# Dots of the second network's first two units made by TensorE from turned rows instead of by VectorE, in a two-network graph kernel

## The reference

```
h = relu(layernorm(x)); x = x + elu(softmax(mask(leaky(f1[:,None] + f2[None,:]))) @ h)
                        # f1, f2 = h @ W_fc.T @ a1, a2
y = relu(layernorm(x))
for l in range(3):
    si = y @ attn_w[l, :256]; sj = y @ attn_w[l, 256:]       # the dots
    attn = softmax(mask(leaky(si[:, None] + sj[None, :] + attn_b[l])))
    h = layernorm(y + attn @ y) * g1[l] + beta1[l]
    y = layernorm(h + gelu(h @ W1[l] + b1[l]) @ W2[l] + b2[l]) * g2[l] + beta2[l]
out = x + y
```

## Time and profile before

| | us |
|---|---|
| median of 3 runs (lowest, highest) | 2795.41 (2794.3, 2795.49) |
| profiled execution, its own time | 2794.51 |
| its span | 2792.7 |
| TensorE busy | 2668.0 (96%) |
| VectorE busy | 2301.8 (82%) |
| ScalarE busy | 2147.8 (77%) |
| GpSimd busy | 1692.1 (61%) |

### The profile page before, as it was taken

How to read it: one execution, slowest core, us unless ns; L and a number is a source line. 1 busy time by engine, 2 the same in 40 slices (tenths; PEclk the granted TensorE clock), 3 DMA queues, 4 the chain that set the end, 5 groups by cost and what they waited for, 6 DMA issues and landing times.

```text
span 2792.7 us, 53529 instructions
## 1 busy us (share of the span) xinstructions
PE 2668.0 (96%) x16868; PEld 2390.7 (86%) x16868; DVE 2301.8 (82%) x8507; ACT 2147.8 (77%) x3982; POOL 1692.1 (61%) x2197
## 2 busy tenths in 40 slices
PE   3599999999999999999999999999999999999997
PEld 2388989898888898898888898989888999999997
DVE  5999888889888888888888888888988777777774
ACT  4588888878787878787877787878777876776774
POOL 4656655656766565666666665655666644544655
PEclk7599999999999999999999999999999999999999
DMA  6221122212222221222221212121323111111111
GB/s 188 93 75 54 65 76 65 71 61 86 83 96 69 66 73 52 80 65 83 79 97 59 80 65 76 56 80 45 102 80 99 54 52 52 35 52 52 50 63 53
DMA packets 118014, 201.34 MB, mean 72 GB/s; under 512 B 12736, under 2 KB 85472, under 8 KB 117728
## 3 DMA queue, kind: packets, MB, share of 16 engines
q1 hardware_dynamic: 117728, 197.87, 21.8%
HBM read 113.95 MB, written 83.89 MB: 71 GB/s over the span
## 4 chain that ended last, share of the span: by engine, by line
PE 70%; DVE 14%; POOL 7%; issue 5%; ACT 3%; DMA 0%; DVEq 0%; POOLq 0%; SPq 0%; ACTq 0%
PE bank L569 33%; PE bank L554 26%; PE ps_u L528 5%; DVE g_lo L917 3%; DVE st L891 3%; POOL xo L358 3%; PE ps_u L610 2%; PE ps_s L523 2%; POOL rs L1198 2%; DVE ub L972 1%; POOL hb L358 1%; DVE ub L1002 1%; PE ps_s L515 1%; DVE vb L886 1%; ACT g_hi L792 1%
## 5 line engine op out<-in xcount | busy, mean ns | idle before, releaser
L569 PE MATMUL bank<-w_hi,g_hi 128*128 128x256 f32 x3072 | 891.7, 290 | 19.0 <-DVE g_lo L917 18.2
L569 PE MATMUL bank<-w_hi,g_lo 128*128 128x256 f32 x3072 | 865.0, 282 | 0.0
L569 PE MATMUL bank<-w_lo,g_hi 128*128 128x256 f32 x3072 | 863.6, 281 | 0.0
L792 ACT ACTIVATE g_hi<-bank,b_eff 128x512 fp32r<-128x512 f32 x768 | 529.0, 689 | 432.8 <-PE bank L554 427.4
L917 DVE TENSOR_TENSOR g_lo<-bank,g_hi 128x512 fp32r<-128x512 f32 x768 | 517.7, 686 | 178.3 <-ACT bank L794 165.7
L554 PE MATMUL bank<-zt_hi,w_hi 128*128 128x512 f32 x1536 | 646.6, 421 | 7.1 <-DVE g_lo L917 3.7
L554 PE MATMUL bank<-zt_hi,w_lo 128*128 128x512 f32 x1536 | 607.1, 395 | 0.0
L554 PE MATMUL bank<-zt_lo,w_hi 128*128 128x512 f32 x1536 | 606.1, 395 | 0.0
L569 PEld LDWEIGHTS bank<-w_hi,g_hi 128*128 128x128 f32 x3072 | 578.5, 188 | 30.5 <-DVE g_lo L917 29.2
L569 PEld LDWEIGHTS bank<-w_lo,g_hi 128*128 128x128 f32 x3072 | 579.1, 189 | 0.8
L569 PEld LDWEIGHTS bank<-w_hi,g_lo 128*128 128x128 f32 x3072 | 578.3, 188 | 0.0
(11 more groups left out here) (95 smaller groups left out, 4291.7 us busy)
## 6 DMA issues: line engine op xcount, KB each, us to landing
xb<-x_scratch SPq DMA_DIRECT2D x88, 512.0 KB, 4.0
x_scratch<-xo SPq DMA_DIRECT2D x64, 512.0 KB, 4.8
xin<-in_x SPq DMA_DIRECT2D x40, 512.0 KB, 4.6
r_scratch<-elu_r SPq DMA_DIRECT2D x32, 512.0 KB, 3.1
xin<-r_scratch SPq DMA_DIRECT2D x32, 512.0 KB, 4.6
out<-xo SPq DMA_DIRECT2D x32, 512.0 KB, 3.3
m<-m_scratch SPq DMA_DIRECT2D x96, 128.0 KB, 3.7
x_scratch<-h SPq DMA_DIRECT2D x24, 512.0 KB, 2.9
```

Source lines behind the costliest of these rows:

```text
L569: mm = pe.matmul(y, g[:, c, r * P:(r + 1) * P], w[:, l, c, :], start=(c == 0 and n == 0), stop=(c == C - 1 and n == 2))
L792: act.activation(g_hi[:, c, :], block_in, ACT.Gelu, bias=bias).then_inc(g_hi_ready, 1)
```

## The change

The dots of units 0 and 1 (steps -3 and -2) are no longer made by VectorE's eight instructions each. TensorE transposes the eight 128 x 128 blocks of the new rows into `bank[0]` and `bank[2]`, ScalarE copies them to SBUF (into `ub`, under the name `ht`), TensorE multiplies them with a two-column operand `aw_col`, and VectorE copies the 8 resulting columns to `dots`. VectorE's copy is put behind its `mask_sums` and `low_halves`. Two loads of 256 single elements each are added for `aw_col`, ahead of the raw weights of layer 0. All later units keep VectorE's dots.

```diff
+        aw_col = sb("aw_col", [P, K1, 2])
...
+        def turned_dots(s):
+            return s < -1
+        def turned_set(s):
+            return s + 3
+        ht = ub.rearrange("p t d -> p (t d)").rearrange("p (k n) -> p k n", k=K1)
...
                 sp.dma_start(b1_col[:, :, :], b1.rearrange("l (c p) -> p l c", p=P),
                              allow_slow_non_contiguous=True).then_inc(const_in, 16)
+                for j in range(2):
+                    sp.dma_start(aw_col[:, :, j], attn_w[0, j * D:(j + 1) * D].rearrange("(k p) -> p k", p=P),
+                                 allow_slow_non_contiguous=True).then_inc(const_in, 16)
                 raw_weights(0)
...
-                pe.wait_ge(const_in, 16 * 3)
+                pe.wait_ge(const_in, 16 * 5)
...
+                def turned_rows(rows, vec, n):
+                    for k in range(K1):
+                        for t in range(T):
+                            mm = pe.transpose(bank[2 * k][:, t * P:(t + 1) * P], rows[:, t, k * P:(k + 1) * P],
+                                              ident[:, :])
+                    mm.then_inc(ht_ps, 1)
+                    pe.wait_ge(ht_ready, K1 * (n + 1))
+                    for t in range(T):
+                        for k in range(K1):
+                            mm = pe.matmul(bank[1][:, 2 * t:2 * t + 2], ht[:, k, t * P:(t + 1) * P], vec[:, k, :],
+                                           start=(k == 0), stop=(k == K1 - 1))
+                    mm.then_inc(hdots_ps, 1)
+                def next_turned():
+                    if turned_dots(s) and live(s + 3):
+                        pe.wait_ge(x_made, st.nth0(s + 3))
+                        if live(s + 2):
+                            pe.wait_ge(dots_ready, st.nth(s + 2, 2 * T))
+                        turned_rows(xb[(s + 3) % 2], aw_col, turned_set(s))
...
                     if -4 <= s <= -2:
                         bias_shifts(s + 4)
+                    next_turned()
                     row_turns()
                     turns()
...
-                act.wait_ge(const_in, 16 * 3)
+                act.wait_ge(const_in, 16 * 5)
...
+                def turned_rows():
+                    if turned_dots(s) and live(s + 3):
+                        n = turned_set(s)
+                        act.wait_ge(ht_ps, n + 1)
+                        if n:
+                            act.wait_ge(hdots_ps, n)
+                        for k in range(K1):
+                            act.activation(ht[:, k, :], bank[2 * k][:, :], ACT.Copy).then_inc(ht_ready, 1)
...
                     elus()
+                    turned_rows()
                     turned()
                     if -4 <= s <= -2:
                         high_halves(s + 4)
...
+                def turned_copy(dot, n, ready):
+                    dve.wait_ge(hdots_ps, n + 1)
+                    dve.tensor_copy(dot[:, :, :], bank[1][:, 0:2 * T].rearrange("p (t j) -> p j t", j=2)).then_inc(
+                        ready, 2 * T)
                 def next_dots(graphs):
-                    if live(s + 3):
+                    if live(s + 3) and turned_dots(s):
+                        turned_copy(dots[(s + 3) % 2], turned_set(s), dots_ready)
+                    elif live(s + 3):
...
                     elu_sums()
-                    next_dots(range(T))
-                    if sums_early:
+                    if turned_dots(s) and sums_early:
                         mask_sums(v0)
                     if -4 <= s <= -2:
                         low_halves(s + 4)
+                    next_dots(range(T))
+                    if not turned_dots(s) and sums_early:
+                        mask_sums(v0)
                     return
```

More of the change, by code:

```diff
@@ L195, in build @@
         v_ps = sem("v_ps")
+        ht_ps = sem("ht_ps")
+        ht_ready = sem("ht_ready")
+        hdots_ps = sem("hdots_ps")
         pro = sem("pro")
@@ L532, in body @@
                 s = st.s
-                v1, v2 = middle(s), late(s)
+                v0, v1, v2 = early(s), middle(s), late(s)
                 l = layer(s)
```

## The result

The changed kernel took 2806.51 us (median of 6 runs, 2805.16 to 2808.18) against 2795.19 for the kernel before (2794.3 to 2796.22): 1.004 times, 95% interval 1.003 to 1.005. So it is 0.4% slower, and outside the range of the prediction, which said 2791.6.

A forecast was written before the change was run, and what follows sets the result against it. TensorE, busy 96% of the span, was taken as the bound, with VectorE bounding the fill. 3.75 + 0.8 - 0.7 = 3.85 us earlier, carried to the end from 2795.41, gave 2791.6 us; range 2788.0 to 2795.8.

The forecast's parts named there:

- the last of the sum: From the end of the fill to the kernel's end: the 3.85 us gained is carried through unchanged.
- C: Step -4: each new single-element load stalls the queue 2.61 us, 5.2 in all; slower, 2796.1 us; chance 0.07.
- D: Step -2: turned path not hidden, GpSimd at 1.6 throughout, root 3.6 us late; time 2796.0 us; chance 0.06.
- E: Step 0: clock rise stays in time while work moves forward, up to 3 us back; about 2794.5 us; chance 0.05.
- if what is gained by 137 us is not what is gained at the end: After the fill: a stated sign that the prediction is wrong, with no size given.
- Step -4, 0.7 lost: The two added loads ahead of the raw weights delay x and VectorE's statistics: 0.7 us lost, bounds 0 and 1.1.
- Step -3, 3.75 gained: Unit 0: without VectorE's dots the score reduction starts at 76.4 instead of 80.14, 3.75 us gained, bounds 3.2 and 4.3.
- Step -2, 0.8 gained: Unit 1: GpSimd's low halves and mask decide, root for unit 0 at 112.8 instead of 113.39; 0.8 gained, bounds -0.1 and 2.3.
- the narrow products: TensorE's eight products for the dots: 1.3 us with hand-overs, bounds 0.95 and 1.97, priced by the bias products.
- ScalarE's wait ahead of `turned`: Step -2: ScalarE stands 2.4 us for unit 0's weight turns; its high halves start at 99.8 instead of 96.11.

The follow-up runs named there:

- first kernel: Changed kernel with `aw_col` allocated behind all other SBUF tensors, so every other tensor keeps its address of the kernel before: 2792.58 us (0.9992).
- eighth kernel: As the seventh kernel, with the two `aw_col` loads issued at step -3 behind layer 1's raw weights, with their own semaphore: 2788.39 us (0.9975).
- seventh kernel: Changed kernel with `aw_col` last and unit 0's weight turns and their copies ahead of unit 1's turned rows: 2788.11 us (0.9978).
- the sixth: Changed kernel with `aw_col` last, only unit 0's dots from turned rows, unit 1's dots on VectorE in the old order: 2794.67 us (0.9999).
- fifth: Kernel before with 32 unused bytes ahead of `w1_hi`, so weights, g and zt all move together: 2794.76 us (0.9999).
- eleventh: Changed kernel with 32 unused bytes ahead of `w1_hi`, the first tensor: 2806.71 us (1.0041).
- ninth: The seventh kernel with 64 unused bytes ahead of `g_hi` and 64 more ahead of `zt_hi`: 2772.1 us (0.9915).
- tenth: Kernel before with only 64 unused bytes ahead of `g_hi` and 64 more ahead of `zt_hi`: 2778.64 us (0.9937).

## Why the prediction was wrong

**The step that failed** is the last of the sum: "From there all engines start by the same amount earlier, and I take it to the end unchanged", with its ground at the start, "The change touches no instruction from step -1 on, so that part can only start earlier or later". It touches no instruction, but it does touch their operands' addresses. That costs 0.217 us in each of the last 16 steps (26.440 - 26.223), 0.083 in the longer ones from unit 23 to 79, and the whole is the difference between the changed kernel and the same with `aw_col` last: 2806.51 - 2792.58 = 13.9 us. None of the rivals had it. C and D looked for a loss in the fill, where the loads cost 0.4 to 1.0 us and step -2 gave 1.0 less than forecast. E is taken up below.

The prediction had named this as a sign of being wrong ("if what is gained by 137 us is not what is gained at the end"), but gave it no price and no chance.

**Without that**, the forecast of 2791.6 stands beside 2792.58. That looks better than it is. The sum said 3.85 us earlier at the end of the fill, and the traces show 1.8 (changed kernel) and 2.3 (first kernel), about half; the median gained 2.4, with an interval from 4.8 faster to 0.6 slower. So the terms erred too, some against each other. From the trace of the changed kernel:

- *Step -4, 0.7 lost.* The statistics start 0.65 us later (37.33), of which 0.26 was there from the first TensorE product on. At step -3 the lag behind the kernel before is 1.16, since the x of that step landed later by half a microsecond. Six traces with this part unchanged have the statistics at 36.51 to 36.94, six with the loads added at 37.10 to 37.42. The eighth kernel puts the loads' price at 0.8. The term is about right; the half microsecond at step -3 was not in the sum.
- *Step -3, 3.75 gained.* From the last elu sum to the score reduction it takes 7.02 us (69.85 to 76.87); before, 11.45 (68.69 to 80.14). Gained: 4.4. The low halves took 1.60 and 1.30 where I took 1.70 each. But 1.3 of it is given back at once: from the reduction to the making of unit 1's rows the changed kernel takes 11.67 us, the kernel before 10.39. GpSimd's low halves end at 81.2, as before (81.5) and as forecast ("near 80 to 82"). But VectorE's small operations come 3.3 us sooner and now run beside them, and a 128x4 operation with two SBUF inputs takes 0.64 us there and 0.16 when they are over (L908 above). The working had no price for that. Net 3.1.
- The Trainium skill says of the port pair that VectorE and GpSimd share that it "is an **exclusive lock**, not a bandwidth split" ("SBUF — State Buffer", section SBUF: two separate sides): each waits for the whole of the other's instruction. The trace agrees for these: the three operations from 77.85 us on came every 0.69 us, which is one GpSimd instruction (5.52 us for 8). It does not agree for GpSimd's mask behind them, a single instruction of 1.93 us from 81.44: beside it one such operation took 0.59 and the next two 0.16 each, so they did not wait for its end. The measurement decides; what differs in the mask stays open.
- *Step -2, 0.8 gained.* Measured: 0.2 lost. The lead was 1.99 us when unit 1's rows were begun (88.54 against 90.53) and 1.82 at the shift (112.81 against 114.63). The mis-sized term is the narrow products, 3.57 us instead of 1.3, which makes ScalarE's copy and all behind it about 2 us late; GpSimd's low halves, 7.43 where the working had 8.5, gave 1.1 of that back. Two errors are in it. The 32 records of the bias products are 16 products of the program (8 chunks by 2 halves), two records each, and not 32 products as "The kernel before" says, so that eight products make 16 records. And the bias products ran at nearly full clock, 0.119 us a record; these ran at the low level, 0.223. The windows of the kernel before and of the changed kernel (after the busy times: granted clock, DMA share, GB/s):

```profile
54.30:58.10 3.80, 3.80 (x33) 3.73 (x31) 1.46 (x4) 2.14 (x8) 3.73 (x6) 0.93 1.01 318
```

```profile
70.50:74.00 3.50, 3.13 (x15) 3.13 (x15) 2.37 (x4) 3.50 (x5) 3.38 (x3) 0.50 0.77 310
94.50:98.40 3.90, 3.56 (x17) 3.56 (x18) 0.61 (x2) 0.29 (x1) 3.14 (x4) 0.50 0.00 0
```

  TensorE had been idle for 7.9 us ahead of the transposes in the first case, and the clock was at 1.2 GHz. A run of these products alone at either level was not made.
- *What was right there:* the order of events. ScalarE's wait ahead of `turned`, the late high halves, GpSimd's low halves (7.43 us, between the bounds of 5.50 and 9.4) and its mask as what the root waits for. The seventh kernel shows that wait's price: removed, unit 1's copy comes 3.6 us earlier (5.88 against 2.28).

**The rival on the clock** (E) said that the rise to full clock in step 0 would stay where it is in time. It moved with the work, from the 3 us after 134 (0.65) to the 3 us after 131 (0.63), after which the changed kernel ran at 1.00. Windows of the kernel before and of the changed kernel:

```profile
134.00:137.00 3.00, 3.00 (x10) 2.37 (x10) 3.00 (x11) 0.00 (x0) 1.28 (x2) 0.65 0.29 108
```

```profile
134.00:137.00 3.00, 2.95 (x18) 2.36 (x18) 3.00 (x11) 1.86 (x3) 0.00 (x0) 1.00 0.85 263
```

What the clock did cost came in single spells later. The changed kernel lost 1.5 us between units 5 and 6 that the kernel before did not. In the chain its first 24 products there took 4.37 us against 2.84, and the granted clock was 0.76 in those 7 us:

```profile
257.00:264.00 7.00, 5.13 (x31) 5.08 (x31) 4.99 (x29) 5.09 (x10) 3.95 (x5) 0.76 0.05 19
```

The kernel before had such a spell at 1481 to 1489 us (0.79), where the changed kernel had none. With one each, they cancel in this pair of traces and explain nothing of the 11 us. Other kernels had theirs elsewhere, and the sixth a longer one of 2.8 us, so a difference of 1 to 3 us between two single traces can be this alone.

## What to carry to other kernels

When a kernel is bound by TensorE for most of its time, adding an SBUF tensor can change the time of every product with one operand ahead of it and one behind. Allocate new tensors last, or keep the distance of stationary and moving operands, and compare the time of one steady step and not only of the part that was edited. And before blaming an edit, run the kernel before with nothing but an unused tensor of that size.

For a price that is taken from a nearby row: count the program's products against the records, and read the granted clock of both stretches.

## What the runs showed of the hardware

TensorE's rate for these products of 128 x 128 by 128 x 256 and by 128 x 512 in fp32r goes by the distance in SBUF between the network's weights and what is allocated behind them, g and zt above all, so most directly by the distance between the operand it loads as weights and the operand it streams: 72 products take 8.48 to 8.63 us, 36 products 8.23 to 8.43, with instructions, order and clock the same (granted 1.00 from 2500 to 2600 us), and moving both operands together changes nothing (the fifth and eleventh kernels). Over the kernel before with unused tensors alone this spans 2778.6 to 2810.6 us, 1.1%. The Trainium skill says that TensorE has two independent SBUF read ports and that loading the next weights does not steal read bandwidth from the running product ("TensorE: Matmul & The Clock Gate", section Step-by-step: what each phase is for). No run here tests that by itself. A rate that changes with the distance alone is not what two wholly independent reads would lead one to expect, but the runs do not show where the time goes.

Distance is not all that enters. In the last unit of the kernel, in a stretch in which ScalarE has no instruction, 24 products of g by the weights take 2.84 us in the kernel before and in the first kernel, but 2.88 in the fifth and seventh, at the same distance, and 2.72 in the ninth and tenth, against 2.85 (before) and 2.82 (ninth, tenth) in the steady steps. What else enters was not followed.

What rule the distances follow stays open. 32 bytes more were bad for both, 64 good for g and slightly bad for zt, 128 good for zt (always with g at 64). Weights, `hi` and `lo` parts lie at different distances, and these were always moved together. That the cause is a clash of two reads in SBUF is a guess: the runs show only that the rate changes with the distance.
